# Tokens stationary in the second product of a transformer tower's last feed-forward layer

## The reference, cut to what matters

```python
h1 = layer_norm(x, ln1_g, ln1_b)
u  = gelu(h1 @ ternary(w1).T + b1)            # 576 x 1024
y  = layer_norm(u, ln2_g, ln2_b) @ ternary(w2).T + b2
return x + y                                  # 576 x 256, rows are tokens
```

## Time and profile before

| | us |
|---|---|
| median of 3 runs (429.53 to 431.42) | 430.42 |
| the profiled execution, its own time | 425.62 |
| its span, first to last instruction | 423.8 |
| PE busy in the span | 397.4 |
| DVE busy | 206.1 |
| ACT busy | 147.7 |
| POOL busy | 104.1 |

### The profile page before, as it was taken

How to read it: one execution, slowest core, us unless ns; L and a number is a source line. 1 busy time by engine, 2 the same in 40 slices (tenths; PEclk the granted TensorE clock), 3 DMA queues, 4 the chain that set the end, 5 groups by cost and what they waited for, 6 DMA issues and landing times.

```text
span 423.8 us, 6446 instructions
## 1 busy us (share of the span) xinstructions
PE 397.4 (94%) x2482; PEld 334.1 (79%) x2482; DVE 206.1 (49%) x438; ACT 147.7 (35%) x314; POOL 104.1 (25%) x126
## 2 busy tenths in 40 slices
PE   8999999999999989999899998986999888999895
PEld 5787887888778889989799898984867555679783
DVE  0347688888945334253333424320213997435452
ACT  1045666666315212121111212110164444346542
POOL 2014544454311731120202202022010040003440
PEclk9999999999996999999899999996999999999989
DMA  7999992000000247768376574013600000000001
GB/s 236 354 318 283 354 394 84 1 2 0 2 0 2 67 115 290 227 141 300 49 291 184 164 236 107 2 19 58 223 0 2 0 2 2 2 0 2 0 2 56
DMA packets 31348, 48.43 MB, mean 114 GB/s; under 512 B 2128, under 2 KB 28368, under 8 KB 29264
## 3 DMA queue, kind: packets, MB, share of 16 engines
q1 hardware_dynamic: 28944, 45.17, 32.7%
q0 software_dynamic: 2368, 2.80, 4.4%
HBM read 38.90 MB, written 9.05 MB: 113 GB/s over the span
## 4 chain that ended last, share of the span: by engine, by line
PE 74%; DMA 8%; DVE 7%; issue 4%; ACT 4%; SPq 2%; POOL 1%; POOLq 0%
PE bank L747 14%; PE bank L617 14%; PE bank L764 10%; DMA wg<-slots 7%; PE bank L499 6%; PE bank L494 4%; PE bank L513 4%; PE bank L973 3%; PE bank L565 2%; PE bank L832 2%; PE bank L894 2%; PE bank L598 2%; PE bank L535 2%; PE bank L959 1%; PE bank L882 1%
## 5 line engine op out<-in xcount | busy, mean ns | idle before, releaser
L747 PE MATMUL bank<-tt,wup 128*128 128x192 f32 x512 | 88.6, 331 | 0.7 <-ACT tt L1090 0.7
L747 PEld LDWEIGHTS bank<-tt,wup 128*128 128x128 f32 x512 | 84.7, 193 | 0.9 <-issue 0.9
L1428 DVE TENSOR_TENSOR scratch<-bank,scratch 128x192 f32<-128x192 f32 x64 | 22.8, 356 | 88.0 <-ACT scratch L1105 88.0
L457 POOL DMA_INDIRECT mixed<-wg,token x16 | 22.6, 1412 | 116.3 <-DVE wg L1442 113.9
L617 PE MATMUL bank<-gru_x,wg 128*128 128x288 f32 x192 | 50.8, 408 | 0.0
L1105 ACT ACTIVATE scratch<-bank 128x192 f32<-128x192 f32 x64 | 21.2, 331 | 73.0 <-PE bank L747 73.0
L410 POOL TENSOR_TENSOR rm<-ve,half_neg 96x3 f32<-96x3 f32 x24 | 21.0, 874 | 96.5 <-DVE ve L1257 89.7
L617 PEld LDWEIGHTS bank<-gru_x,wg 128*128 128x128 f32 x192 | 35.5, 190 | 8.8
L429 POOL TENSOR_TENSOR sq<-sq 128x288 f32<-128x288 f32 x14 | 26.0, 1855 | 23.9 <-ACT sq L1021 23.9
L494 PE MATMUL bank<-zero 128*128 128x288 bf16 x155 | 26.5, 323 | 4.7 <-issue 3.5
L494 PEld LDWEIGHTS bank<-zero 128*128 128x128 bf16 x155 | 16.7, 111 | 11.1 <-issue 3.7
(11 more groups left out here) (217 smaller groups left out, 644.0 us busy)
## 6 DMA issues: line engine op xcount, KB each, us to landing
wup<-w_up SPq DMA_DIRECT2D x8, 2048.0 KB, 8.9
wdn<-w_down SPq DMA_DIRECT2D x8, 1024.0 KB, 6.7
slots<-empty SPq DMA_DIRECT2D x2, 2385.0 KB, 20.2
wg<-w_gru SPq DMA_DIRECT2D x4, 1024.0 KB, 10.8
wup<-w SPq DMA_DIRECT2D x2, 1024.0 KB, 9.3
wg<-slots SPq DMA_DIRECT2D x16, 99.4 KB, 5.3
xp<-w_qkv SPq DMA_DIRECT2D x1, 1536.0 KB, 16.8
xp<-patches SPq DMA_DIRECT2D x2, 432.0 KB, 6.1
```

What stands on the lines that cost most here:

```text
L457: pool.indirect_dma_start(out=mixed, out_offset=bass.IndirectOffsetOnAxis(ap=token[i][:, u:u + 1], axis=0), in_=yw[i][:, u, :], in_offset= ...
L747: last = pe.matmul(bank[:, 2 + m % 4, g * 256:g * 256 + C], wup[i][:, k, g * I + m * P:g * I + (m + 1) * P], xg[i][:, k, :], start=(k == 0 ...
L1428: dve.tensor_tensor(gt[m % 2], bank[:, 2 + m % 4, 0:C], sg[m % 2], ALU.mult).then_inc(s_vact[c], 1)
```

## The change

The second product is turned round. Each chunk's `gy` is multiplied by the gain and split by DVE into two fp32r parts (`split_hidden`, two instructions per q). These parts, 96 tokens at a time, are the stationary operand, and `q2` (256 columns, exact in fp32r) is the moving one: six matmuls per q, into one bank per token tile. Rows of tokens come out, so mean and root are numbers per partition: `take_mean` and `close` are one DVE instruction per tile each, and nothing is spread or turned at the end. The input rows `h` are transposed inside the loop instead (`rows_out`), copied by ACT (`keep_rows`), and POOL adds the shift row to them (`add_shift`). The products of gain and shift are formed as 96 equal rows (`shift_rows`). POOL no longer makes `w2`. The second half's layer norm moves into the loop, DVE's share of it between the steps q = 0 to 6. `b2` is loaded as a broadcast by one DMA of its own, next to last of SP's first list. `out_var(0)` goes from behind the sum of q = 10 to that of q = 11.

```diff
-        OUTWARD = {2: (0,), 3: (1,), 5: (2,), 6: (3,), 8: (4,), 9: (5,), 10: (6,), 12: (7,)}
+        OUTWARD = {3: 0, 4: 1, 5: 2, 6: 3, 7: 4, 8: 5, 9: 6, 11: 7, 12: 8, 14: 9, 15: 10}
...
+        parts = sb("parts", [P, 4, 2, NT], F32R)
+
+        def part(q, c):
+
+            slot = q % 4 if q < KI else (q - KI + 4) % 6
+            return parts[:, slot, c, :] if slot < 4 else (xh, xl)[c][0][:, slot - 4, :]
...
-                sp.wait_ge(s_trc, j + 1)
+                sp.wait_ge(s_fin, j + 1)
                 sp.dma_start(out[j * TT:(j + 1) * TT, :], oc[:, j, :]).then_inc(s_out, 16)
...
-            pool.wait_ge(s_q2, 1)
-            for k in range(KI):
-                pool.tensor_tensor(w2[:, k, :], q2[:, k, :].bitcast(F32),
-                                   vec[:, V_GB2 + 2 * k:V_GB2 + 2 * k + 1].broadcast_to([P, H]), ALU.mult).then_inc(s_gam, 1)
             for i in range(LN_MLP, LN_OUT):
                 power(i)
+            def add_shift(g):
+                pool.wait_ge(s_htc, g + 1)
+                pool.wait_ge(s_gb, 1)
+                rows = base[:, 2 * g:2 * g + 2, :]
+                pool.tensor_tensor(rows, rows, brow[:].rearrange("p (o n) -> p o n", o=1).broadcast_to([TT, 2, H]),
+                                   ALU.add).then_inc(s_base, 1)
+
...
                         pool.wait_ge(s_acc, n * (KI - 1) + m - 1)
                     pool.tensor_tensor(to, gsq[n][:, 0, :] if m == 1 else to, gsq[n][:, m, :], ALU.add)\
                         .then_inc(s_acc, 1)
+                    if n == 1 and m in (1, 3, 5):
+                        add_shift(m // 2)
                 power(i)
...
-                pe.wait_ge(s_stc, i - LN_OUT)
-                pe.wait_ge(s_gb, 1)
+                if i == LN_OUT:
+                    pe.wait_ge(s_gb, 1)
+                else:
+                    pe.wait_ge(s_less, 1)
                 for c, src in enumerate((ysum[i % 2], sq[i % 2][:, 0, :])):
                     for j in range(JT):
-                        last = pe.matmul(bank[0:TT, 4, c * JT + j:c * JT + j + 1], src[:, j * TT:(j + 1) * TT], mean_i[:],
+                        last = pe.matmul(bank[0:TT, sums_bank(i % 2), c * JT + j:c * JT + j + 1], src[:, j * TT:(j + 1) * TT], mean_i[:],
                                          start=True, stop=True)
...
-            def shift_products(pairs, warm=True):
+            def shift_rows(at):
 
                 pe.wait_ge(s_q2, 1)
                 pe.wait_ge(s_ve, LN_MLP + 1)
-                for m, k in pairs:
-                    if warm:
-                        stay_warm(1, 1)
-                    for part in (vh, vl):
-                        last = pe.matmul(bank[:, 4, 2 * m:2 * m + 2], q2[:, k, m * P:(m + 1) * P],
-                                         part[:, k, :], start=(k == 0 and part is vh), stop=(k == KI - 1 and part is vl))
-                    if m == KH - 1 and k == KI - 1:
+                for c, k in at:
+                    for v in (vh, vl):
+                        last = pe.matmul(bank[0:TT, 4, c * H:(c + 1) * H], v[:, k, c:c + 1].broadcast_to([P, TT]), q2[:, k, :],
+                                         start=(k == 0 and v is vh), stop=(k == KI - 1 and v is vl))
+                    if k == KI - 1:
                         last.then_inc(s_gbp, 1)
...
-            pairs = [(m, k) for m in range(KH) for k in range(KI)]
-            project(1, 0)
-            pe.wait_ge(s_oc, NAT)
+            shifts = [(c, k) for c in range(2) for k in range(KI)]
+            project(1, 0, range(2))
             ln_square(LN_MLP)
+            project(1, 0, range(2, 4))
+            ln_spread(LN_MLP)
             project(1, 1)
-            ln_spread(LN_MLP)
-            shift_products(pairs[:2])
-            pe.wait_ge(s_ha, 2)
-            ln_mean(LN_MLP + 1, h[:, :, half(1)])
-            shift_products(pairs[2:5])
-            pe.wait_ge(s_cen, LN_MLP + 2)
-            shift_products(pairs[5:7])
-            ln_square(LN_MLP + 1)
-            stay_warm(3, 1)
+            shift_rows(shifts[:5])
...
-            def outward(q):
+            def outward(q, tiles=range(JT)):
                 n, k = q // KI, q % KI
-                if n == 0:
-                    pe.wait_ge(s_gam, k + 1)
-                pe.wait_ge(s_gel, q + 1)
+                pe.wait_ge(s_split, q + 1)
                 if q == 0:
+                    pe.wait_ge(s_ha, 2)
+                    pe.wait_ge(s_cen, LN_MLP + 2)
+                if q == KI:
+                    pe.wait_ge(s_stc, 1)
+                    pe.wait_ge(s_htc, 3)
                     pe.wait_ge(s_norm, spreads(LN_MLP + 1))
-                if q == KI:
-                    pe.wait_ge(s_norm, spreads(LN_OUT))
-                for m in range(KH):
-                    last = pe.matmul(bank[:, 2 + m, 0:NT], w2[:, k, m * P:(m + 1) * P], gy[n][:, k, :],
-                                     start=(k == 0), stop=(k == KI - 1))
-                if k == KI - 1:
-                    last.then_inc(s_w2, 1)
+                for j in tiles:
+                    to = bank[0:TT, tile_bank(n, j), 0:H]
+                    for c in range(2):
+                        last = pe.matmul(to, part(q, c)[:, j * TT:(j + 1) * TT], q2[:, k, :],
+                                         start=(k == 0 and c == 0), stop=(k == KI - 1 and c == 1))
+                return last
+
+            def rows_out(g):
+                if g == 0:
+                    pe.wait_ge(s_norm, spreads(LN_MLP))
+                else:
+                    pe.wait_ge(s_htc, g)
+                for u in range(2):
+                    t = 2 * g + u
+                    for m in range(KH):
+                        last = pe.transpose(bank[0:TT, 5, u * H + m * P:u * H + (m + 1) * P],
+                                            h[:, m, t * TT:(t + 1) * TT], ident[:])
+                last.then_inc(s_ht, 1)
...
             for q in range(2 * KI):
                 hidden(q)
                 if q == 1:
+                    pe.wait_ge(s_ha, 2)
+                    ln_mean(LN_MLP + 1, h[:, :, half(1)])
+                    shift_rows(shifts[5:10])
+                elif q == 2:
+                    shift_rows(shifts[10:])
+                elif q == 5:
                     ln_spread(LN_MLP + 1)
-                if 1 <= q <= 3:
-                    shift_products(pairs[4 + 3 * q:7 + 3 * q], False)
-                for before_it in OUTWARD.get(q, ()):
-                    outward(before_it)
-                if q == KI + 1:
+                if q in OUTWARD:
+                    outward(OUTWARD[q]).then_inc(s_ow, 1)
+                if q == 3:
+                    ln_square(LN_MLP + 1)
+                elif q in (6, 8, 10):
+                    rows_out(q // 2 - 3)
+                if q == 10:
                     close(0)
-                if q == KI + 3:
-                    ln_spread(LN_OUT)
-            for q in range(KI, 2 * KI):
-                outward(q)
-                if q == KI + 2:
-                    close(1)
-                if q == KI + 5:
-                    ln_spread(LN_OUT + 1)
-            stay_warm(4)
-
-            for n in range(2):
-                pe.wait_ge(s_fin, n + 1)
-                for j in range(JT):
-                    t = n * JT + j
-                    if t >= 2:
-                        pe.wait_ge(s_trc, t - 1)
-                    for m in range(KH):
-                        last = pe.transpose(bank[0:TT, t % 2, m * P:(m + 1) * P],
-                                            h[:, m, t * TT:(t + 1) * TT], ident[:])
-                    last.then_inc(s_tr, 1)
+            outward(11)
+            outward(12)
+            close(1)
+            outward(13)
+            for j in range(JT):
+                outward(14, (j,))
+                outward(15, (j,)).then_inc(s_tile, 1)
...
-            squares(LN_MLP + 1)
-
-            def mean_part(n):
-
-                sc_.wait_ge(s_gb, 1)
-                sc_.wait_ge(s_bc, spreads(LN_OUT + n))
-                for m in range(KH):
-                    last = sc_.activation((zz, tt)[n][1][:, m, :], bank[:, 6, 0:NT], ACT.Identity, scale=gb[:, m, 0:1],
-                                          bias=gbn[:, m:m + 1])
-                last.then_inc(s_mg, 1)
+
+            def keep_rows(g):
+                sc_.wait_ge(s_ht, g + 1)
+                sc_.activation(base[:, 2 * g:2 * g + 2, :], bank[0:TT, 5, 0:2 * H].rearrange("p (t n) -> p t n", n=H),
+                               ACT.Copy).then_inc(s_htc, 1)
 
             for n in range(2):
                 for m in range(KI):
                     q = n * KI + m
-                    if q == KI + 5:
-                        mean_part(0)
                     sc_.wait_ge(s_u, q + 1)
                     sc_.activation(gy[n][:, m, :], bank[:, m % 2, 0:NT], ACT.Gelu, scale=wsi[:, 0:1],
                                    bias=vec[:, V_B1 + m:V_B1 + m + 1]).then_inc(s_gel, 1)
                     sc_.wait_ge(s_gel, q + 1)
```

(111 more changed lines are left out.)

55 lines of the change are left out of this document (28 added, 27 removed).

## The result

Four executions of the changed kernel have a median of 436.38 us (435.24 to 439.62), four of the kernel before, beside them on the same chip, 430.92 (429.53 to 433.57). Some executions of any kernel are a few per cent slow, so ratios here compare fast ones: 1.0193 times, 95% interval 1.0147 to 1.0239, where the two medians alone give 1.0127. It is slower. The forecast said 435.9 in a range of 428.5 to 439.0, 5.5 us or 1.0127 times, slower with a chance of 0.68.

The account below looks back on a forecast made before the run. PE was taken to bound the old ending, then DVE, PE and ACT in turns. 3.9 us at full clock plus 1.6 for the clock, 5.5, made 425.6 into 431.1; with 4.8 to the median 435.9 us, range 428.5 to 439.0.

Parts of the forecast that it names:

- Steps 1 to 5: Changed stretch at full clock, from the earlier start to the tail: last close at 425.5, 3.9 us slower.
- turns: Second half, POOL and DVE excluding each other from the first root on: 12.0 us, last sum ends at 418.4.
- The hand-over of 0.14: Where DVE waits for POOL: DVE starts its real work 0.14 us before POOL's instruction ends.
- The chain's "12 instructions": End of the old kernel's chain of waits: eight outward products read as 12 instructions in 2.91 us.
- the price of 0.243: Old second product on PE: 0.243 us per fp32 instruction, 15.6 us for 64.
- add_shift: POOL's second half: three instructions of 96x512, taken at 1.2 us each between bounds of 0.64 and 1.40.
- The split's parts: DVE's two split instructions per q: 0.31 us for the first, 0.46 for the second.
- The first root: POOL's first root comes late: starts at 406.5 instead of 399.96, after POOL idles for 10 us.
- The tail at full clock: From the last sum to the last close: 7.1 us instead of 4.7.
- The step that failed is 6: Half clock behind PE's two idle stretches of 5 and 7 us: costs 1.6 us, bounds 0 and 3.4.
- Rival (a): Loop's two halves: POOL costs DVE nothing, last close at 420.1, 1.5 us faster, 428.9 us; chance 0.27.
- Rival (b): POOL and DVE turns without overlap add 3.2 us and nearly 1, or fp32r costs like fp32: 439.9; chance 0.10.

Follow-up runs that it names:

- e3: Changed kernel with idle PE kept busy by bf16 matmuls of zeros, 34 before hidden(8) and 54 before the last sums: 432.51 us, 1.0026 times the kernel before.
- e6: Changed kernel with the fourteen POOL additions of squares replaced by memsets that read nothing (variance wrong): 425.15 us, 1.0036 times the kernel before.
- e4: Changed kernel without six of seven POOL additions of squares in each half (mean square wrong): 428.53 us, 0.9927 times the kernel before.
- e1: Changed kernel as it is, a second time: 436.88 us, 1.0127 times the kernel before.
- e14: Changed kernel unchanged, on the same chip as e13: 430.16 us (two executions), 1.0149 times the kernel before.
- e2: Changed kernel with the first half's sums directly after hidden(8) and its variance after the sum of q = 9 instead of 11: 437.93 us, 1.0158 times before.
- e13: Kernel before the change, unchanged, on the same chip as e14: 422.54 us.
- e10: e4 with 14 and 26 filler products in PE's two idle stretches: 419.51 us, 0.9918 times the kernel before.
- e5: Kernel before the change, unchanged, profiled a second time: 422.76 us against 423.64 for the same kernel, 0.9989.
- e11: Kernel before the change with 15 filler products on PE ahead of the spread of the first half's statistics: 421.02 us, 0.9953 times the kernel before.
- e12: Changed kernel with squares summed on PE by one-column products spread among large products, first tile's mean taken earlier: 427.78 us against 428.69 before, 0.9952.
- e7: Changed kernel with squares summed on PE, 24 one-column products per half in one block, instead of POOL additions: 428.5 us, 1.0131 times the kernel before.

## Why the prediction was right, and where it was wrong

**Steps 1 to 5 at full clock: right.** e3 is the execution they describe, since its clock holds. On the scale of the trace before, its last close ends at 369.32 + 55.91 = 425.2 us; the text said 425.5. In detail, from the profile after on the same scale: hidden(0) at 379.9 (forecast 379.7), hidden(8) at 397.8 (397.4) with 4.66 us of idle time ahead of it (nearly 5), turns of 11.88 us (12.0), idle time ahead of the last sums 7.27 (since 411: 7.4). Outward products start 0.113 us apart (2.22 us for 18, less a fill of 0.3), as taken (0.11). The hand-over of 0.14 held: 0.13 in the pair above.

**Terms that were off and cancelled.** The chain's "12 instructions" are three of the eight outward products, not all; the price of 0.243 and the sum don't change by it. add_shift takes 1.30 to 1.36 us in e6 and 1.39 in e4, near the upper bound of 1.40, where I took 1.2. The split's parts are 0.37 and 0.52, not 0.31 and 0.46: 16 x 0.12 = 1.9 us more DVE work, of which the wait for ACT's Gelu hid a part. The first root came 1.7 us later than forecast, 0.7 of it at full clock (e3). The tail at full clock took 6.1 us (e3: 49.82 to 55.91), not 7.1.

**The step that failed is 6.** It gave the clock 1.6 us; e3 shows 2.9, near its upper bound of 3.4. "Such an idle stretch needn't be followed by a fall at the worst place": it was, behind both idle stretches, in every profile of the changed kernel (after, e1, e14: 0.50 to 0.59 over the first products) and in e2. The mechanism and the places were right, the size was not. The forecast end of the stretch, 58.4 + 1.6 = 60.0, stood against 61.13, a difference of 5.5 against 6.65 to 7.0. The ratio of 1.0193 would make it 8.3 us; what that has over the stretch lies ahead of it, where nothing was forecast (3.55 us in the two first profiles, 1.2 in e13 and e14), and its cause stays open. That the total came out 0.5 us from the median (435.9 and 436.38) owes something to luck: the medians moved by 5.5 us here, by 4.9 in e1 and by 6.8 in e14 (430.16 against 423.35), the stretch by 6.7 to 7.0.

**Rival (a), POOL and DVE hardly meet,** is refuted by the sums of 751 instead of 451 ns and by e4. It said 1.5 us faster than before for a POOL that costs DVE nothing, and e4 is 1.8 shorter, but that is no proof of its sum: (a) kept POOL's queue of 10.1 us, and e4 took most of it away. e6 comes nearer to (a)'s case and is 3.0 us longer than before, though its first split parts still wait and its clock fell. **Rival (b), no overlap at the hand-over,** is refuted by the 0.13 of overlap and by the turns' 11.88 us; fp32r products at fp32's price by 0.113 us.

**The change has a gain in it.** With POOL's additions left out and the clock kept (e10) its stretch is 51.86 us, 1.5 shorter than before with its clock kept (e5, e11: 53.35); with nothing left out 0.7 of it is kept (e12). What made it slower is where the squares were left: POOL's additions mostly fell in DVE's gaps before (5.7 us ahead of the sums), and the change filled the gaps.

## What to carry to other kernels

Before DVE gets more work, count what GpSimd reads from SBUF in the same stretch: where DVE's instructions have two inputs in SBUF the two are one resource, so add their times, and see whether the sum fits (here twelve POOL additions of 0.8 us cost the end 6.3 us, and 8.4 with the clock). Moving the start of one of them gained nothing (e2); taking its work to a third engine did, if it is laid between large products (e12) and not in a block (e7). Price a new idle stretch of TensorE with the half clock behind it, and look for what waits on the slowed products.

## What the runs showed of the hardware that was not expected

The granted clock can fall while PE is busy. In e7 it is 1.00 up to 394 us, falls to 0.50, its lower level of 1.2 GHz, within the first block of one-column fp32 products, and stays there while PE is busy for 3.20 of 3.20 us. That block stands behind an idle stretch of 0.68 us, but the second block stands behind none, and the same happens:

```profile
414.22 4.39 PE L555 MATMUL bank<-mean_i,gru_y 128*96 128x1 f32 x48
418.47 1.10 PE L542 MATMUL bank<-mean_i,scratch 128*96 128x1 f32 x6
```

The clock is 1.00 up to 417 us and 0.50 from 418, so the six products of L542 take 1.10 us instead of the 0.65 of e12. Spread between products of 256 and 288 columns, as many of them leave the clock at 1.00 from the first, at 388 us, to behind the last, at 415.5 (e12). Such an instruction takes 0.09 us at full clock and 0.145 at half; whether the load of 96 columns or the product sets this wasn't tried apart.
